# Gathers beside the last batch: at most two under way

## The chip, the cores and the metric

The kernel runs on one core of a Trainium2 chip. The metric is the time of one execution on the device in microseconds, as a median of several runs. Before the change it is 834.48 us (three runs, 833.97 to 837.61). TensorE (PE) multiplies matrices, VectorE (DVE) and ScalarE (ACT) work element by element, GpSimd (POOL) does small element work and issues the gathers, SyncE (SP) issues most other DMAs.

## The reference

A decoder layer on x of 16 x 56 x 256 (batch, tokens, channels): a linear self-attention, a cross-attention over 1500 context rows with 16 heads, and a feed-forward with routed experts. Each is added to its input and normalised. The part whose data the change concerns is the feed-forward:

```python
rows = mask_idx // H          # 2048 entries
cols = mask_idx % H
vals = jnp.einsum('tk,tks->ts', rw, weighted[top_idx])
xg = xt[:, cols]              # the gather
contrib = jax.ops.segment_sum((xg * vals).T, rows, num_segments=H)
out = xt @ W.T + contrib.T
```

For each of 2048 entries a channel of x (`cols`) is picked for all tokens, multiplied by the routed value of token and entry, and added into the channel `rows`.

## The kernel before

Cross-attention goes batch by batch (b = 0 to 15). A batch has eight head pairs t, taken in four duos. For each pair TensorE transposes the probabilities in three groups of four tiles (L1179, `transposes`), ScalarE copies group 0 and 2 out of PSUM (L1300), and so does VectorE with group 1 in the last batch (L1427); then come TensorE's products with the values (L1193). In between stand the scores of pair t+2 (L1157), VectorE's masked copy of them (L1396) and ScalarE's exponentials (L1288). The copies wait for `values_done` (the values two pairs back) and for their group of transposes in `probsT_in_psum`, both counted up by TensorE. In all batches but the last, TensorE also projects the context of the next batch; the last has room, and there the first half of the tokens (448 of 896) is made ready for the feed-forward. Its x, transposed, is stored to DRAM as `x2T[0]` by ScalarE (L677).

The gathers read that store. The feed-forward works in 16 tiles of 128 entries (j = 0 to 15, `NST` = 16) for each half h of the tokens. Gather j is an indirect DMA that GpSimd issues (L683): it fetches 128 rows of 448 floats, 1792 bytes each and 229,376 in all, into the buffer `xg[j]`. Two neighbouring gathers count up one semaphore, `xg_in[j // 2]`, by 16 each. There is one set of sixteen buffers, filled for h = 0 beside the last batch (L1099 to L1107) and refilled for h = 1 during the feed-forward, each as soon as its product has been read (L1722 to L1724). Buffers 0 to 8 lie in the room of the projections, 9 to 14 in that of the values, 15 in that of the stacked keys, and so the loop waits, on GpSimd, before j = 3 (`k_in`, all key transfers), before j = 9 (`values_done`) and before j = 15 (`scores_in_psum`).

The feed-forward begins with TensorE finishing the last tile's attention output (`late_unit_on_tensor`, L741 and L747, with VectorE between and behind) and the first value products (L1753). For each n = 16 h + j VectorE waits for `xg_in` and for the value product and multiplies them (L1898), ScalarE rounds (L1840), GpSimd or VectorE takes the rest (L1712, L1888), and TensorE scatters the two parts into the channels (L1762). GpSimd's first instruction in this block is the memset of `c_stack1` (L1705).

Of the kernel before, what the change touches and what calls it, by code (L numbers as in the profile page):

```python
# [573 lines left out]
def units_before(half, a):  # L574

    if isinstance(half, int) and half == 0:
        return NU * (1 + a)
    return half * NU2 + NU - NR + a * (NU + NR)
# [40 lines left out]
def expert_room(keep):  # L619

    room = {"room": keep["room"][:], "context": keep["context"][:], "w": keep["wkvT"][:].rearrange("p k m d -> p (k m d)"),
            "v": keep["v_sb"][:, 0].rearrange("p l d -> p (l d)")}
    at = dict.fromkeys(room, 0)

    def take(which, cols, rows=P, dt=None):
        view = room[which][0:rows, at[which]:at[which] + cols]
        at[which] += cols
        return view.bitcast(dt) if dt else view  # L630

    return {
        "pick_r": split(take("room", NST * D), NST),
        "c_stack": take("room", HALF),
        "xg": [take("room", HALF, dt=F32) for j in range(XG_ROOM)] + [take("v", HALF) for j in range(XG_ROOM, NST - 1)]
        + [keep["k_stack"][:].rearrange("p k l -> p (k l)")[:, 2 * BUFS * HALF:(2 * BUFS + 1) * HALF].bitcast(F32)],
        "x2T": split(take("context", 2 * KT * HALF), 2 * KT),
        "x2T_hi": split(take("w", KT * HALF), KT),
        "x2T_lo": split(take("w", KT * HALF), KT),
        "c_lo": take("context", T, rows=E, dt=F32R),  # L640
        "channel_row": take("context", D),
        "col_i": take("context", NST, dt=I32),
        "idx_col": take("context", NST, dt=I32),
        "row_i": take("context", NST, dt=I32),
        "row_f": take("context", NST),
        "expert_row": take("context", E, rows=TT),
    }
# [16 lines left out]
def shares_stack(keep, h):  # L664
    return expert_room(keep)["c_stack"] if h == 0 else keep["c_stack1"][:]
# [14 lines left out]
def gather_on_gpsimd(nc, pool, io, keep, h, j):  # L680

    e = expert_room(keep)
    nc.gpsimd.indirect_dma_start(e["xg"][j], None, io["x2T"][h], bass.IndirectOffsetOnAxis(ap=e["col_i"][:, j:j + 1], axis=0)  # L683
                                 ).then_inc(keep["xg_in"][j // 2], 16)
# [12 lines left out]
def result_on_gpsimd(nc, pool, keep, tile):  # L697
    pool.wait_ge(keep["var_ready"], tile + 1)
    t = slice(tile, tile + 1)
    nc.gpsimd.tensor_tensor(keep["rstd"][:, t], keep["var_eps"][:, t], keep["minus_half"][:, t], ALU.pow).then_inc(keep["rstd_ready"], 1)  # L700

def tables_on_gpsimd(nc, pool, keep):

    e = expert_room(keep)
    channels = keep["channels"]
    nc.gpsimd.iota(e["channel_row"], pattern=[[1, D]], base=0, channel_multiplier=0,
                   allow_small_or_imprecise_dtypes=True).then_inc(channels, 1)
    nc.gpsimd.iota(e["expert_row"], pattern=[[1, E]], base=0, channel_multiplier=0,
                   allow_small_or_imprecise_dtypes=True).then_inc(channels, 1)  # L710
# [186 lines left out]
def cross_attention_phase(nc, io, keep):  # L897
    ctx = ExitStack()
    with ctx:
# [73 lines left out]
        def readers_done(b, c):  # L973

            if b == 1:
                return last_reader(AT_FIRST, c) + 1
            half, a = (b - 2) // 2, b % 2
            return units_before(half, a) + last_reader(AT if a or half == 0 else AT_R, c) + 1
# [5 lines left out]
        with nc.Block() as block:  # L984
# [81 lines left out]
            @block.gpsimd  # L1066
            def _(pool):
                def split_context(b):
                    for c in range(NC):
                        e = slice(c * LC, (c + 1) * LC)  # L1070
                        pool.wait_ge(ctx_in[c], 16 * (b + 1))
                        pool.wait_ge(unit_in_psum, readers_done(b, c))
                        nc.gpsimd.tensor_copy(cT_hi[:, :, e], context[:, :, e]).then_inc(ctx_hi, 1)  # L1073
                        pool.wait_ge(ctx_hi, NC * b + c + 1)
                        nc.gpsimd.tensor_tensor(cT_lo[:, :, e], context[:, :, e], cT_hi[:, :, e].bitcast(F32), ALU.subtract).then_inc(ctx_lo, 1)  # L1075

                for part, (raw, hi, lo) in enumerate(((w_raw, "wT_hi", "wT_lo"), (gate_raw, "gateT_hi", "gateT_lo"))):
                    pool.wait_ge(wT_hi_ready, part + 1)
                    nc.gpsimd.tensor_tensor(keep[lo][:], raw, keep[hi][:].bitcast(F32), ALU.subtract).then_inc(keep["wT_lo_ready"], 1)
                pool.wait_ge(load["bias"], 32)  # L1080
                nc.gpsimd.tensor_tensor(x1[:], x1[:], bo_row.unsqueeze(1).broadcast_to([TT, NT, D]), ALU.add).then_inc(x1_bo_ready, 1)
                nc.gpsimd.memset(keep["minus_half"][:], -0.5).then_inc(keep["half_set"], 1)
                pool.wait_ge(keep["half_set"], 1)
                for a in range(2):
                    split_context(1 + a)
                for i in range(NT - 2):
                    for a in range(2):
                        split_context(2 * i + 3 + a)
                    result_on_gpsimd(nc, pool, keep, i)
                split_context(B - 1)  # L1090
                pool.wait_ge(ctx_lo, NC * B)
                tables_on_gpsimd(nc, pool, keep)
                result_on_gpsimd(nc, pool, keep, NT - 2)

                pool.wait_ge(keep["col_ready"], 1)
                pool.wait_ge(unit_in_psum, units_before(last, 1))
                nc.gpsimd.memset(shares_stack(keep, 0).bitcast(F32), 0.0).then_inc(keep["stack_cleared"], 1)
                pool.wait_ge(keep["x2T_stored"][0], 16)
                for j in range(NST):  # L1099
                    if j == XG_EARLY:  # L1100
                        for p in range(NP):
                            pool.wait_ge(k_in[p], 16 * STACK * B)
                    if j == XG_ROOM:
                        pool.wait_ge(values_done, (B - 1) * NP + 2)
                    if j == NST - 1:
                        pool.wait_ge(scores_in_psum, (B - 1) * NP + 3)
                    gather_on_gpsimd(nc, pool, io, keep, 0, j)  # L1107

            @block.tensor
# [857 lines left out]
```

## Time and profile before

| | us |
|---|---|
| median of the runs | 834.48 |
| lowest, highest | 833.97, 837.61 |
| profiled execution | 835.97 |
| its span | 834.2 |
| TensorE busy | 741.3 (89%) |
| VectorE busy | 513.1 (62%) |
| ScalarE busy | 505.9 (61%) |
| GpSimd busy | 224.4 (27%) |

Times in the rows are microseconds from the start of the span. A row of the instruction list gives start, duration, engine, line, operation, output and inputs, shape, count, and in brackets the idle time of the engine before it with what ended it. "remote" there means that the trace shows no engine of this core as the one that released it, "issue" that it shows nothing that was waited for. The granted clock of TensorE is 1.00 at 2.4 GHz and 0.50 at 1.2 GHz. Matmul ends are modelled, and some matmul records can be missing. An issue of a gather counts as busy on GpSimd only as long as the instruction itself runs; its data moves later on queue q0.

### The profile page before, as it was taken

How to read it: one execution, taken by the hardware profiler on the slowest of the kernel's cores; microseconds unless marked ns; L12 is line 12 of the kernel's file. 1: busy time of each engine (PE TensorE's matmuls, PEld its weight loads, DVE VectorE, ACT ScalarE, POOL GpSimd, SP SyncE). 2: the span in 40 equal slices, each digit the busy share in tenths (PEclk: the TensorE clock that was granted, in tenths of full speed). 3: DMA queues.
4: the chain of work that ended last, by engine and by line, in shares of the span. 5: the costliest groups of instructions: out<-in, count | busy, mean ns of one | idle time of the engine just before them, and what ended most of it. 6: DMA issues, size and time to landing. Idle time of an engine off the chain costs nothing. (4 is left out here: it accounts for less than half of the span.)

```text
span 834.2 us, 18337 instructions
## 1 busy us (share of the span) xinstructions
PE 741.3 (89%) x7341; PEld 621.4 (74%) x7341; DVE 513.1 (62%) x993; ACT 505.9 (61%) x846; POOL 224.4 (27%) x176
## 2 busy tenths in 40 slices
PE   5745599999999999999999999999999999647954
PEld 2434388888888888888888888888888888436743
DVE  2886755565665566657656655666566556735655
ACT  4304157776677676767775776677677767523323
POOL 1020340413133131404040504051313310433633
PEclk9775899999999999999999999999999999959978
DMA  9008977887777778877887788778877755830421
GB/s 231 34 4 249 217 186 178 191 194 194 161 186 161 186 166 203 178 187 165 203 177 189 166 204 177 192 169 199 195 162 186 165 112 121 200 97 2 131 70 44
DMA packets 59891, 134.19 MB, mean 161 GB/s; under 512 B 24936, under 2 KB 43080, under 8 KB 59720
## 3 DMA queue, kind: packets, MB, share of 16 engines
q1 hardware_dynamic: 55632, 124.31, 63.9%
q0 software_dynamic: 2048, 7.34, 3.3%
q10 hardware_dynamic: 2128, 1.38, 0.6%
q8 instruction: 59, 0.97, 0.5%
q14 instruction: 24, 0.20, 0.1%
HBM read 53.50 MB, written 5.57 MB: 71 GB/s over the span
## 5 line engine op out<-in xcount | busy, mean ns | idle before, releaser
L1300 ACT ACTIVATE probsT<-ps_T 125x448 f32<-125x448 f32 x376 | 190.8, 541 | 160.1 <-PE ps_T L1179 144.9
L1396 DVE CUSTOM_DVE_ANT_0 scores<-ps_scores,mask_sb 112x1500 f32<-112x1500 f32 x128 | 219.7, 1717 | 94.6 <-PE ps_scores L1157 86.7
L1179 PE MATMUL ps_T<-ident,scores 112*128 112x112 f32 (+1 forms) x1536 | 196.5, 264 | 18.6 <-ACT probsT L1300 16.1
L1179 PEld LDWEIGHTS ps_T<-ident,scores 112*128 112x128 f32 (+1 forms) x1536 | 169.9, 146 | 54.1 <-ACT probsT L1300 36.9
L1288 ACT ACTIVATE scores<-scores,shift 112x1500 f32<-112x1500 f32 x128 | 197.0, 1541 | 3.7 <-DVE shift L1396 3.1
L1145 PE MATMUL ps_proj<-wkvT,room 128*125 128x256 f32 x1152 | 160.1, 288 | 0.0
L1138 PE MATMUL ps_proj<-room,wkvT 128*128 128x500 f32 x576 | 150.0, 406 | 8.4 <-DVE room L1483 8.4
L1073 POOL CAST room<-ctx_rows 128x1000 fp32r<-128x1000 f32 x45 | 45.8, 1019 | 401.1 <-PE ps_proj L1138 400.5
L1145 PEld LDWEIGHTS ps_proj<-wkvT,room 128*125 128x125 f32 x1152 | 141.8, 186 | 8.9 <-issue 8.1
L1138 PEld LDWEIGHTS ps_proj<-room,wkvT 128*128 128x128 f32 x576 | 106.7, 194 | 27.2 <-issue 8.7
L1157 PE MATMUL ps_scores<-k_stack,q_stack 96*112 96x500 f32 x384 | 118.1, 415 | 2.4 <-issue 1.7
L1075 POOL TENSOR_TENSOR room<-ctx_rows,room 128x1000 fp32r<-128x1000 f32 x45 | 105.5, 2345 | 3.6
L1379 DVE COPY v_sb<-ps_proj 125x512 f32<-125x512 f32 x96 | 66.0, 688 | 62.8 <-PE ps_proj L1145 62.8
L1383 DVE SCALAR_TENSOR_TENSOR room<-ps_proj,xbk,room 128x500 fp32r<-128x500 f32 x96 | 70.9, 739 | 51.2 <-ACT room L1283 50.1
L1193 PE MATMUL ps_out<-probsT,v_sb 125*32 125x112 f32 x3072 | 88.6, 263 | 1.9 <-DVE probsT L1427 1.9
L1283 ACT ACTIVATE room<-ps_proj,xbk 128x500 fp32r<-128x500 f32 x96 | 64.7, 674 | 42.2 <-PE ps_proj L1138 23.8
L1193 PEld LDWEIGHTS ps_out<-probsT,v_sb 125*32 125x32 f32 x3072 | 72.6, 111 | 16.9 <-issue 10.7
L1157 PEld LDWEIGHTS ps_scores<-k_stack,q_stack 96*112 96x112 f32 x384 | 58.1, 178 | 11.6 <-issue 3.6
L1840 ACT ACTIVATE k_stack<-prod 128x448 fp32r<-128x448 f32 x32 | 18.2, 579 | 42.5 <-DVE prod L1898 40.3
L1762 PE MATMUL psC<-k_stack,room 128*128 128x448 f32 x128 | 33.6, 392 | 3.0 <-POOL k_stack L1712 2.9
L281 PE MATMUL psA<-xT,wT 128*128 128x448 f32 x48 | 22.7, 638 | 12.2 <-DMA xT<-in_xT 6.8
L1762 PEld LDWEIGHTS psC<-k_stack,room 128*128 128x128 f32 x128 | 25.0, 201 | 7.5 <-POOL k_stack L1712 4.4
(246 smaller groups left out, 489.5 us busy)
## 6 DMA issues: line engine op xcount, KB each, us to landing
k_stack<-room SPq DMA_DIRECT2D x384, 187.5 KB, 3.9
ctx_rows<-in_ctx SPq DMA_DIRECT2D x48, 500.0 KB, 5.6
mask_sb<-in_mask_BxSxS_ff SPq DMA_DIRECT2D x32, 328.1 KB
q_stack<-q_hi SPq DMA_DIRECT2D x32, 112.0 KB, 5.3
q_hi<-k_stack SPq DMA_DIRECT2D x4, 448.0 KB, 3.8
q_lo<-k_stack SPq DMA_DIRECT2D x4, 448.0 KB, 4.0
q_stack<-q_lo SPq DMA_DIRECT2D x16, 112.0 KB, 5.3
xT<-in_xT SPq DMA_DIRECT2D x2, 448.0 KB, 7.9
```

The costliest lines, as they stand in the source:

```text
L1075: nc.gpsimd.tensor_tensor(cT_lo[:, :, e], context[:, :, e], cT_hi[:, :, e].bitcast(F32), ALU.subtract).then_inc(ctx_lo, 1)
L1138: last = nc.tensor.matmul(ps_proj[:, bank, 0:LC], w, x, start=i == 0, stop=i == len(mm) - 1)
L1145: last = nc.tensor.matmul(ps_proj[0:LT, bank, j * D:(j + 1) * D], w, x, start=i == 0, stop=i == len(mm) - 1)
L1157: last = nc.tensor.matmul(ps_scores[0:PN, c, 0:LC], q_stack[:, a, t], k_stack[0:STACK * PD, t, c * LC:(c + 1) * LC], start=True, stop=True)
L1179: last = nc.tensor.transpose(ps_T[0:wide, (TB * t + k) % 2, j * PN:(j + 1) * PN], scores[:, t % 2, key:key + wide], keep["ident"][0:PN, 0:PN])
L1193: last = nc.tensor.matmul(ps_out[k * PD:(k + 1) * PD, d * PN:(d + 1) * PN], v_sb[0:LT, a, j, t * PD:(t + 1) * PD], probsT[:, t % 2, j], st ...
L1283: nc.scalar.activation(k_hi[:, q * LC:(q + 1) * LC], src, ACT.Identity, bias=keep["xbk"][:, p:p + 1]).then_inc(hi_ready, 1)
L1288: nc.scalar.activation(scores[:, t % 2], scores[:, t % 2], ACT.Exp, scale=-1.0, bias=shift[:, t % 2:t % 2 + 1], accum_out=keep["sums"][:, ...
L1300: nc.scalar.activation(probsT[:, t % 2, k * TC:(k + 1) * TC], ps_T[0:LT, (TB * t + k) % 2, 0:TC * PN].rearrange("p (j n) -> p j n", j=TC), ...
L1379: nc.vector.tensor_copy(v_sb[0:LT, a, 2 * p:2 * p + 2], split(ps_proj[0:LT, bank], 2)).then_inc(unit_out, 1)
L1383: nc.vector.scalar_tensor_tensor(out=k_lo[:, c], in0=ps_proj[:, bank, 0:LC], scalar=keep["xbk"][:, p:p + 1], in1=k_hi[:, c].bitcast(F32), ...
L1396: nc.vector.tensor_tensor_reduce(out=split(scores[:, t % 2], NC), in0=ps_scores[0:PN, :, 0:LC], in1=split(mask_sb[:, a], NC), scale=-1.0, ...
```

## The change

In the loop of the first sixteen gathers GpSimd waits, before every even j from 2 on, until both gathers of the pair ahead have landed.

```diff
@@ -1104,6 +1104,8 @@
                         pool.wait_ge(values_done, (B - 1) * NP + 2)
                     if j == NST - 1:
                         pool.wait_ge(scores_in_psum, (B - 1) * NP + 3)
+                    if j % 2 == 0 and j > 0:
+                        pool.wait_ge(keep["xg_in"][j // 2 - 1], 32)
                     gather_on_gpsimd(nc, pool, io, keep, 0, j)
 
             @block.tensor
```

The loop of the second sixteen (L1722) is not touched.

## Rows read from the trace of the kernel before

**Rows 1.** Busy time in stretches: stretch, length, engines, clock, DMA share, GB/s.

```profile
core 0: us, PE busy (x) PEld busy (x) DVE busy (x) ACT busy (x) POOL busy (x), PEclk, DMA share, GB/s
716.00:722.80 6.80, 5.69 (x42) 4.12 (x40) 5.04 (x14) 3.22 (x6) 3.12 (x3) 1.00 0.92 226
722.80:727.00 4.20, 2.59 (x57) 2.04 (x57) 3.96 (x22) 3.53 (x5) 3.22 (x4) 1.00 0.44 115
727.00:741.40 14.40, 2.19 (x6) 0.92 (x5) 0.00 (x0) 0.00 (x0) 9.20 (x10) 0.52 0.65 175
741.40:751.00 9.60, 8.69 (x75) 7.04 (x76) 6.77 (x20) 5.38 (x10) 0.00 (x0) 0.50 0.01 2
```

**Rows 2.** GpSimd's instructions in order of time, first run of gathers (16).

```profile
716.40 1.22 POOL L683 DMA_INDIRECT room<-x2T,ctx_rows  x1 [2.28 <-DMA x2T<-ctx_rows]
...
719.18 0.95 POOL L683 DMA_INDIRECT room<-x2T,ctx_rows  x1 [0.30 <-issue]
722.86 0.94 POOL L683 DMA_INDIRECT room<-x2T,ctx_rows  x1 [2.74 <-DMA k_stack<-room]
724.11 0.95 POOL L683 DMA_INDIRECT room<-x2T,ctx_rows  x1 [0.30 <-issue]
...
738.00 0.95 POOL L683 DMA_INDIRECT k_stack<-x2T,ctx_rows  x1 [0.30 <-issue]
```

**Rows 3.** TensorE, ScalarE and VectorE in order of time around the gathers.

```profile
727.06 0.45 PE L1179 MATMUL ps_T<-ident,scores 112*128 112x112 f32 x3 [0.99 <-issue]
...
741.44 0.54 ACT L1300 ACTIVATE probsT<-ps_T 125x448 f32<-125x448 f32 x1 [15.11 <-remote]
741.51 0.62 DVE L1427 COPY probsT<-ps_T 125x448 f32<-125x448 f32 x1 [14.64 <-remote]
```

**Rows 4.** Gather queue in windows 718:722 and 724:727: packets, MB, share.

```profile
q0 software_dynamic: 137, 0.54, 53.8%
...
q0 software_dynamic: 128, 0.46, 58.2%
```

**Rows 5.** The microseconds in which the two runs of gathers run out.

```profile
741.00:742.00 1.00, 0.00 (x0) 0.00 (x0) 0.49 (x1) 0.54 (x1) 0.00 (x0) 0.50 0.00 0
...
800.00:801.00 1.00, 0.00 (x0) 0.00 (x0) 0.00 (x0) 0.00 (x0) 0.00 (x0) 0.50 0.13 50
```

**Rows 6.** Last instruction of the cross-attention block, first of the next.

```profile
755.96 0.54 ACT L1327 ACTIVATE outT<-ps_out 128x448 f32<-128x448 f32 x1 [0.80 <-PE ps_out L1193]
...
756.77 0.47 POOL L1705 MEMSET c_stack<- 128x448 f32 x1 [17.83 <-POOLq L984]
```

**Rows 7.** Second run of gathers and the product that follows it.

```profile
778.03 1.09 POOL L683 DMA_INDIRECT room<-x2T,ctx_rows  x1 [3.30 <-DMA x2T<-ctx_rows]
779.42 1.33 POOL L683 DMA_INDIRECT room<-x2T,ctx_rows  x1 [0.30 <-DVE prod L1898]
...
792.45 0.65 PE L1753 MATMUL psC<-c_stack,w_stack 128*128 128x448 f32 x2 [0.91 <-DMA c_stack<-ctx_rows]
...
797.40 0.95 POOL L683 DMA_INDIRECT k_stack<-x2T,ctx_rows  x1 [0.30 <-issue]
801.03 1.16 DVE L1898 TENSOR_TENSOR prod<-psC,room 128x448 f32<-128x448 f32 x2 [11.74 <-issue]
```

**Rows 8.** Busy time and clock where the clock rises, and in the feed-forward's start.

```profile
751.00:752.00 1.00, 0.81 (x7) 0.61 (x5) 0.60 (x2) 0.91 (x2) 0.00 (x0) 0.79 0.00 0
...
756.70:764.00 7.30, 6.25 (x42) 5.41 (x43) 5.03 (x11) 1.11 (x2) 2.76 (x3) 1.00 0.00 0
...
806.00:807.00 1.00, 1.00 (x6) 0.92 (x6) 0.71 (x2) 0.55 (x1) 0.00 (x0) 0.98 0.00 0
```

**Rows 9.** TensorE's first groups of the feed-forward, and one at half clock.

```profile
756.81 1.76 PE L741 MATMUL psC<-fold,outT 128*112 128x64 f32 x16 [0.95 <-PEq L984]
758.38 0.66 PE L1753 MATMUL psC<-room,w_stack 128*128 128x448 f32 x2
759.64 1.13 PE L747 MATMUL psC<-r_norm,sel 112*112 112x128 f32 x8 [0.60 <-DVE r_norm L802]
...
801.71 1.27 PE L1753 MATMUL psC<-c_stack,w_stack 128*128 128x448 f32 x2 [8.62 <-DVE prod L1898]
```

## The prediction, made blind

> **What bounds the kernel now.** I read the page first. Most of the span is the cross-attention of 16 batches, where TensorE is busy 9 tenths and more of nearly every slice; only the last slices fall below that. The change touches nothing before 716 us, so the whole argument lies behind it. The table of stretches shows the hole: from 727.0 to 741.4 us VectorE and ScalarE do nothing, TensorE 2.19 us, at half the clock, while GpSimd issues and the DMA engines are busy 0.65 of the time [rows 1]. The list of GpSimd's instructions says what that traffic is: sixteen gathers in three runs, j=0 to 2 from 716.40, a pause for `k_in` until 722.86, then thirteen in a row, each 0.95 us long with 0.30 us between, the last at 738.00 [rows 2].
>
> The three compute engines are not waiting for the gathered data, since the first product that reads it stands in the next block. The code says what they wait for: ScalarE's copy L1300 waits for a group of four transposes, VectorE's copy L1427 for the next group. By the list in order of time TensorE ran the last of these by 727.5, yet the copies start at 741.44 and 741.51, and the trace names no engine as releaser ("remote") [rows 3]. They start 3.4 us after the last gather is issued, in the first microsecond that has no DMA traffic [rows 2, 3, 5]. So something in the gathers' stream holds up what TensorE should pass on, and lets go when the stream ends. It happens again in the feed-forward: the second sixteen are issued from 778.03 to 797.40, VectorE's product for the second half has its matmuls by 793.1 and starts at 801.03, when the traffic has just run out [rows 5, 7]. That is the ground for expecting anything from the change. It is no proof that the number under way is the cause: three gathers in a row at 716 to 720 held nothing up, and in the second sixteen the engines worked on for about ten microseconds.
>
> Behind the hole the remaining work of the batch takes from 741.44 to 756.50, and 0.27 us later the next block starts on all engines [rows 3, 6].
>
> **The change, part by part.** It adds seven waits to GpSimd, before j = 2, 4, ..., 14, each for both gathers of the pair ahead. No instruction is removed or moved; the second sixteen gathers keep their own code. The register work of a wait is nothing beside what it waits for. What is new is the length of the train. One gather is 64 packets: the two issued at 722.86 and 724.11 make 128 by 727.0, so the second is through at most 2.9 us after its issue [rows 4]. The last one, issued at 738.00, has its traffic behind it by 741.0, 3.0 us; the engines woke at 3.4 [rows 2, 3, 5]; in the second train 797.40 to a little past 800, 2.8 us or somewhat more [rows 5, 7]. I take 3.2 us from issue to the semaphore. The step between two gathers of a pair is 0.95 + 0.30 = 1.25 us, and GpSimd's return from the wait is the 0.25 or so that its other gaps show. One pair costs 1.25 + 3.2 + 0.25 = 4.7 us, where two gathers cost 2.5 us today. The bounds are 2.8 and 3.4 us of landing, so 4.3 and 4.9 us.
>
> The first wait is nearly free: by 722 the stream has moved 137 packets, so j=0 and j=1 (128) are down, and j=2 starts at about 722.6 instead of 719.18; j=3 has to sit out `k_in` until then anyway [rows 2, 4]. From there the pairs start at 722.6 + 4.7k; the seventh (j=14, 15) at 722.6 + 28.2 = 750.8, the last gather at 752.05, done at 753.0. Behind these waits on GpSimd stands nothing of this block, but the block ends for everyone only when GpSimd is through: the memset L1705, the first thing of the next block, comes 0.27 us after ScalarE's last copy of this one, and TensorE starts with it [rows 6, 9]. So GpSimd, ready at 739 today, becomes the engine that can set the block's end: 753.0 + 0.3 = 753.3, against 756.77 now. Gain 3.5 us; with the bounds of the pair 5.9 down to 2.3 us. The DMA that feeds `xg` is then as far as it was: j=0 is read first, j=15 last, some twenty microseconds later.
>
> The Trainium skill, "DMA: Bandwidth & Descriptors", section on the anatomy of one DMA on the software path, gives about 2.0 us fixed plus bytes over 436e3 per us. For the 229,376 bytes of a gather that is an estimate of 2.5 us, a pair of 4.0 us and a block end 4.2 us earlier than mine; the row with 3.0 us decides, and the sum goes by it.
>
> Do the other engines finish by 753? At 727 they have two duos of the batch left, which took 15.06 us, 9.6 of them at half clock [rows 1, 3]. The window from 724.0 holds all 128 packets of j=3 and j=4, so traffic begins over 1.1 us after an issue [rows 2, 4]; I take 1.4. If every pair holds TensorE's signals from there to its last landing (4.45 us), the gap to the next traffic is 1.65 us, and the engines do another half microsecond before they need a signal: 2.1 to 2.2 of 4.7 us, 46%. From 727 to 753.3 that is 12 us of the 15. If the hold doesn't form with two under way, they are done at about 740. So the end is set by GpSimd or very near it: between 753.3 and some 757.
>
> What comes back is the clock. Today TensorE has worked without a break since 742, its clock rose at about 751.4 and the feed-forward starts at full clock [rows 1, 8]. After the change it idles before the block's end, or limps through it; the clock is 1.00 up to 727.0 and 0.52 on average behind it [rows 1], so it falls soon after TensorE runs dry. Two matmuls of 448 columns took 0.66 us at full clock and 1.27 at half, a factor of 1.9 [rows 9]. The first groups of the feed-forward are on the chain: L741 1.76 us, L747 1.13 us [rows 9]. If the clock comes back some 4.5 us after the restart, as after 801.71 [rows 8, 9], only L741 pays, +1.6 us; if it takes nine, as after 742.0, all of TensorE's 6.25 us up to 764 pays, at most 0.9 x 6.25 less the 1.05 us of slack there, +4.6 us [rows 8]. I take L741 and L747, 0.9 x 2.89 = 2.6 us.
>
> Sum: -3.5 + 2.6 = -0.9 us. The profiled execution took 835.97 us (span 834.2), 1.5 us above the median of the runs, 834.48. Against that median: 833.6 us. The second hole (789 to 801) is left as it is, since its train isn't changed.
>
> **Rivals.**
> (a) Faster. The hold is gone, and the clock costs nothing because TensorE works up to the block's end, or the landings are as quick as the lower bound: 3.5 to 5.9 us gained, with nothing given back. Middle 4.7: 829.8 us. For it: the first three gathers held nothing up. Against it: if the hold is gone TensorE is done long before GpSimd, and then it is cold.
> (b) Slower: the hold isn't lifted between pairs. The traffic pauses only from a landing to the next pair's first packets, 1.65 us, and where the hold ended at 741.44 there was no next gather. If that doesn't do, it lasts until the longer train is over: 752.05 + 3.4 = 755.4, then 15.06 us of work: 770.5 against 756.50, +14.0 us, 848.5 us. It decides from the point where the release takes longer than the pause. For it: the hold's start doesn't follow the count under way. Against it: VectorE resumed within a microsecond of the last traffic.
> (c) Slightly slower: the pairs take over 4.9 us, or the hold eats more of each pair than I took, and the block ends at 757 to 759, cold: 0.2 to 2.2 us later plus the 1.6 to 4.6 us of the clock, +2 to +7, middle +4.5: 839 us. The engines that now run beside the gathers can also slow the issue: in the second train, beside a busy VectorE, the first two issues took 1.09 and 1.33 us where 0.95 is the rule [rows 7].
> (d) The count has no bearing: the hold comes and goes with something else. Then GpSimd ends at 753, the others at 756.5 as now, and nothing changes: 834.5 us. The Trainium skill, "SBUF — State Buffer", section on the two separate sides, says that a DMA can't slow a compute operation, which speaks for this. The trace has 14 us in which all three compute engines stand beside nothing but gathers [rows 1], so I trust the row over the rule as far as waiting goes.
>
> **How the numbers follow.** Forecast (GpSimd sets the end, cold start) 0.42; (a) 0.23; (b) 0.12; (c) 0.15; (d) 0.08. The forecast's own range is 830.2 (5.9 gained, 1.6 paid) to 836.8 (2.3 gained, 4.6 paid). The whole range reaches down to 828.0, (a) with its best 5.9 and half a microsecond below, and up to 842.0, the end of (c); left out are (b) and the rim of (a). Half a percent, 4.2 us, is about what a measurement of this kernel can tell from none. Faster by more: most of (a) and the rim of the forecast, 0.25. Slower by more: (b) and most of (c), 0.24. Between: 0.51.
>
> **What would show it.** Right: gathers in pairs 4.3 to 4.9 us apart from 722.6, GpSimd's last at about 752, L741 at 753.3 with its sixteen matmuls in over 3 us at half clock, and copies L1300 and L1427 spread over the stretch and not bunched at its end. The DMA share falls to zero once per pair. Wrong: L741 behind 757, or one long idle stretch of ScalarE up to the last landing (b); a full clock at L741 (a); a second hole of another length, which I took as constant. What would upset it most is a clock that stays up while the hold is gone, and a second hole that moves.

## The result: slower, and the profile after

The changed kernel takes 839.63 us, median of 17 runs (837.93 to 843.29), against 834.67 us (17 runs, 831.67 to 837.61) for the kernel before on the same chip: a ratio of 1.0056, 95% interval 1.0040 to 1.0071, so it is slower by about half a percent, clear of the noise. Forecast were 833.6 us and no measurable difference, with a range of 828 to 842. The profiled execution has a span of 839.5 us where the one before has 834.2, so the two profiles differ by 5.3 us, about as much as the medians. Lines behind L1106 have moved down by two.

GpSimd's instructions in order of time, kernel after (start, duration, engine, line; in brackets the idle time ahead of it and what ended it):

```profile
716.75 1.25 POOL L683 DMA_INDIRECT room<-x2T,ctx_rows  x1 [2.95 <-DMA x2T<-ctx_rows]
718.30 0.95 POOL L683 DMA_INDIRECT room<-x2T,ctx_rows  x1 [0.30 <-issue]
723.32 0.94 POOL L683 DMA_INDIRECT room<-x2T,ctx_rows  x1 [4.07 <-DMA room<-x2T,ctx_rows]
724.57 0.95 POOL L683 DMA_INDIRECT room<-x2T,ctx_rows  x1 [0.30 <-issue]
728.14 0.94 POOL L683 DMA_INDIRECT room<-x2T,ctx_rows  x1 [2.63 <-DMA room<-x2T,ctx_rows]
...
752.09 0.94 POOL L683 DMA_INDIRECT v_sb<-x2T,ctx_rows  x1 [2.60 <-DMA v_sb<-x2T,ctx_rows]
753.34 0.95 POOL L683 DMA_INDIRECT k_stack<-x2T,ctx_rows  x1 [0.30 <-issue]
757.60 0.47 POOL L1707 MEMSET c_stack<- 128x448 f32 x1 [3.31 <-POOLq L984]
```

The waits are there: two gathers, then GpSimd idles until both have landed, 4.07 us after the first pair and 2.4 to 2.7 us after the others. From 723.32 to 752.09 are six pairs of 4.80 us. Against the train of before [rows 2] it is now 15 us longer. The last line is the first thing of the next block, and it stands 3.31 us behind the end of the last gather's instruction, 4.26 us behind its start.

```profile
L984 POOLq DRAIN  x1: 13648/13648/13648, 728.5 to 728.5; - x1
...
L984 POOLq DRAIN  x1: 5480/5480/5480, 751.9 to 751.9; - x1
```

The record begins before the last gather has been issued. Before, it ends at 742.1, which is 4.1 us behind the last issue and 0.7 us behind the last landing (741.39); nobody waited for it there. After, it ends at 757.35, 4.0 us behind the last issue and again 0.7 us behind the landing (756.64), and the memset follows 0.25 us later.

ScalarE in order of time, kernel after, where the hole was [rows 3]:

```profile
726.42 0.54 ACT L1302 ACTIVATE probsT<-ps_T 125x448 f32<-125x448 f32 x1 [0.41 <-PE ps_T L1181]
727.67 0.54 ACT L1302 ACTIVATE probsT<-ps_T 125x448 f32<-125x448 f32 x1 [0.71 <-PE ps_T L1181]
...
739.16 0.55 ACT L1302 ACTIVATE probsT<-ps_T 125x448 f32<-125x448 f32 x1 [1.12 <-PE ps_T L1181]
741.30 0.54 ACT L1329 ACTIVATE outT<-ps_out 128x448 f32<-128x448 f32 x1 [1.59 <-PE ps_out L1195]
```

The wait of 15.11 us [rows 3] is gone. All of ScalarE's copies go through, none waits more than 2.14 us from 724 us on, those that wait are released by TensorE, and the last copy of the batch starts at 741.30 instead of 755.96 [rows 6]: the three compute engines have finished the batch 14.7 us earlier. And none of it arrives, as the list of TensorE shows:

```profile
739.05 2.14 PE L1195 MATMUL ps_out<-probsT,v_sb 125*32 125x112 f32 x48
757.64 3.22 PE L741 MATMUL psC<-fold,outT 128*112 128x64 f32 x16 [16.44 <-PEq L984]
760.62 1.09 PE L1755 MATMUL psC<-room,w_stack 128*128 128x448 f32 x2
761.93 2.05 PE L747 MATMUL psC<-r_norm,sel 112*112 112x128 f32 x8 [0.21 <-DVE r_norm L802]
```

It waits 16.44 us for the block to end, starts 0.83 us later than before [rows 9], and then does the same three groups at half speed: 3.22, 1.09 and 2.05 us where it was 1.76, 0.66 and 1.13 [rows 9]. The stretches of the kernel after say how long (stretch, length, busy times of PE, PEld, DVE, ACT, POOL, clock, DMA share, GB/s):

```profile
742.00:744.00 2.00, 0.00 (x0) 0.00 (x0) 0.00 (x0) 0.00 (x0) 1.25 (x2) 1.00 0.00 0
744.00:746.00 2.00, 0.00 (x0) 0.00 (x0) 0.00 (x0) 0.00 (x0) 0.64 (x1) 0.53 0.66 170
746.00:757.00 11.00, 0.00 (x0) 0.00 (x0) 0.00 (x0) 0.00 (x0) 3.78 (x4) 0.50 0.33 94
757.00:764.00 7.00, 6.15 (x27) 5.57 (x28) 2.01 (x4) 1.11 (x2) 1.38 (x2) 0.50 0.00 0
764.00:766.00 2.00, 2.00 (x10) 1.81 (x10) 1.81 (x6) 0.00 (x0) 1.36 (x2) 0.85 0.00 0
```

TensorE is out of work at 741, its clock is at the lower of its two levels (1.2 of 2.4 GHz) from about 744, and it comes back at about 765, 7 us after the restart. In the first stretch there is no DMA traffic, although a gather was issued at 742.44.

All the rest can be followed with four marks on each profile: the first gather, the start of the last block (the memset), the first gather of the second sixteen, the end of the span. All runs made for this study in one table (us; distances between the marks, so that it doesn't matter when an execution reached the first one):

| kernel | first gather to block | block to second gathers | second gathers to end | last gather of first train to block |
|---|---|---|---|---|
| before | 40.4 | 21.3 | 56.2 | (18.8) |
| after | 40.9 | 24.8 | 57.1 | 4.26 |
| e1_warm | 40.8 | 20.9 | 56.7 | 4.44 |
| e2_slide | 33.3 | 26.6 | 56.2 | 4.11 |
| e3_drain | 33.3 | 23.2 | 56.1 | (10.7) |
| e4_second | 40.4 | 21.6 | 54.7 | (18.8) |
| e5_endwait | 41.3 | 26.4 | 56.2 | 5.02 |
| e6_inter | 36.7 | 26.7 | 52.5 | (14.5) |
| e7_drain_both | 35.7 | 23.3 | 51.1 | (10.6) |
| e8_triples | 38.0 | 26.6 | 56.2 | 4.09 |
| e9_moved | 34.7 | 26.4 | 56.1 | 4.12 |
| e10_moved4 | 26.5 | 27.0 | 52.0 | 3.89 |

In brackets: the compute engines, not GpSimd, were last at the block's end. From before to after: +0.35 at the first gather itself, +0.48, +3.50 and +0.97, together the 5.3 us.

Each row is one profiled execution. The times of the runs are medians, and each ratio below is to the kernel before on the same chip (835.38 us there for e1 to e4, 835.45 for e5 to e8, 835.70 for e9 and e10); kernels from different groups are compared by these ratios.

### The profile page after: what moved, and what is told of

Same layout as the page of the kernel before. It is cut to its first block and busy times, and to the rows that moved or that the text cites. A ratio compares the mean times of both kernels' runs of the same rounds, so it can differ in the third digit from the quotient of the medians.

```text
span 839.5 us, 18337 instructions
## 1 busy us (share of the span) xinstructions
PE 741.1 (88%) x7341; PEld 622.1 (74%) x7341; DVE 512.6 (61%) x993; ACT 505.8 (60%) x846; POOL 224.2 (27%) x176
## 5 line engine op out<-in xcount | busy, mean ns | idle before, releaser
L1195 PEld LDWEIGHTS ps_out<-probsT,v_sb 125*32 125x32 f32 x3072 | 72.5, 110 | 17.3 <-issue 10.7
```

Source lines behind the costliest of these rows:

```text
L1195: last = nc.tensor.matmul(ps_out[k * PD:(k + 1) * PD, d * PN:(d + 1) * PN], v_sb[0:LT, a, j, t * PD:(t + 1) * PD], probsT[:, t % 2, j], st ...
```

## Experiments

Three questions: what sets the end of the block, what the clock costs, and what makes and lifts the hold. The base of each diff is named, and the diffs are cut to what matters. The runs with `landed` in them (e2, e4, e6, e7, e8, e10) also deal out the semaphores differently: gather j counts up `xg_in[j % 8]`, a train without waits of its own gets one for the gather eight ahead, and the count to wait for is

```
+def landed(h, j):
+    return 32 * h + 16 * (1 + j // 8)
```

`low(n)` is GpSimd's part of the arithmetic for product n.

**e1_warm.** After, and TensorE is kept at work up to the block's end, with 74 matmuls whose result nobody reads:

```
...
+                for _ in range(74):
+                    nc.tensor.matmul(ps_proj[:, 0, 0:HALF], keep["wT_hi"][:, 0, 0:P], ...)
```

> The changed kernel, with 74 matmuls of 448 columns added at the end of TensorE's list for the last batch; they compute nothing that is read and fill the 16 us in which TensorE waits for GpSimd. Theory (the clock): the feed-forward starts at full clock at 757.6 as in the changed kernel, L741 takes 1.8 us and not 3.2, and GpSimd's second gathers begin 21.2 us behind that start, as before the change, and not 24.7. Time 836.0 us against 839.6. Rival (the feed-forward's start lost its 3.5 us to something else than the clock, such as the gathered data arriving late): 839 to 840 us with the clock up.

Measured: 837.87 us (ratio to before 1.0032, 1.0001 to 1.0064). TensorE and the clock (stretch, length, PE busy, clock, DMA share, GB/s):

```profile
741.00:755.00 14.00, 13.70 (x69) 1.00 0.36 100
755.00:764.00 9.00, 8.07 (x52) 1.00 0.00 0
```

The first group of the block is back at its old length:

```profile
754.95 1.76 PE L741 MATMUL psC<-fold,outT 128*112 128x64 f32 x16 [0.30 <-PEq L984]
```

The stretch from block to second gathers shrinks from 24.8 to 20.9 us, so the cold start costs 3.9 us there, and the distance to the block's start, 40.8, stays as it was. TensorE was as busy as can be beside the gathers and the gathers kept their pace. The time shows less: the ratios, 1.0032 against 1.0056, are 2 us apart with overlapping intervals, and 837.87 us is 1.9 over what was expected. So the 3.9 us rest on one profiled execution of each kernel; the stretch is the sharper reading, since it leaves out what varies elsewhere.

**e5_endwait.** After, and GpSimd also waits for the landing of the last pair before it leaves the block:

```
+                pool.wait_ge(keep["xg_in"][NST // 2 - 1], 32)
```

> The changed kernel with one wait more: at the end of its list beside the last batch GpSimd also waits for the last pair of gathers to have landed, before the block ends. Theory 1, the end of the block waits for the landing of the last gather anyway: the added wait takes over what the profile now shows as 3.31 us in front of the memset, the memset still starts about 4.3 us after the last gather's issue (753.34 to 757.60), and the time stays where the changed kernel's is, about 839.6 us. Rival, the 3.3 us are a fixed price of ending a block after gathers that does not depend on the landing: it comes on top, the memset starts about 7.5 us after the last issue, and the time is about 842.5 us.

Measured: 841.63 us (1.0068, 1.0043 to 1.0094), not to be told from the 1.0056 of after. GpSimd, last gather and memset:

```profile
752.35 0.95 POOL L683 DMA_INDIRECT k_stack<-x2T,ctx_rows  x1 [0.30 <-issue]
757.37 0.47 POOL L1708 MEMSET c_stack<- 128x448 f32 x1 [4.07 <-POOLq L984]
```

```profile
L984 POOLq DRAIN  x1: 1380/1380/1380, 755.7 to 755.7; - x1
```

Behind the six pairs ahead of it this wait costs 2.5 to 2.7 us of idle time; here it moved the memset by 0.8 us (5.02 us from the last issue instead of 4.26). So the two overlap: without any wait in the code, GpSimd's block doesn't end before its last gather is down. In the ten other runs besides this one and the changed kernel the DRAIN ends 0.5 to 0.7 us behind the last landing, while from issue to landing it took 3.1 to 3.5 us.

**e9_moved.** After, and the last pair is issued in the next block, behind the memset:

```
-                for j in range(NST):
+                for j in range(NST - 2):
...
+                for j in range(NST - 2, NST):
+                    if j % 2 == 0:
+                        pool.wait_ge(keep["xg_in"][j // 2 - 1], 32)
+                    gather_on_gpsimd(nc, pool, io, keep, 0, j)
```

> The changed kernel with its last pair of gathers (14 and 15) issued behind the memset in the last block instead of beside the last batch. Theory, the end of the block waits for the landing of the last gather of GpSimd's list, and the list is as long as its pairs: the memset starts one pair (4.8 us) earlier after the first gather, 36.0 us instead of 40.85, again about 4.3 us after the last gather beside the batch; ScalarE and VectorE are done at 741 to 742 and don't set it. The pair in the last block lies in GpSimd's idle time before its first low part. TensorE's clock stays at 0.50 at the block's start, so the stretch to the second gathers stays at 24 to 25 us. Time 839.6 less 4.8, about 834.8 us. Rival, the 3.3 us in front of the memset hang on something other than the gathers: the memset moves by less than 2 us and the time is 838 to 840.

Measured: 836.22 us (1.0004, 0.9982 to 1.0027). By the ratios that is about 4 us under after, and the intervals don't touch.

```profile
748.16 0.94 POOL L683 DMA_INDIRECT v_sb<-x2T,ctx_rows  x1 [0.30 <-issue]
752.28 0.47 POOL L1705 MEMSET c_stack<- 128x448 f32 x1 [3.17 <-POOLq L984]
752.95 0.95 POOL L683 DMA_INDIRECT v_sb<-x2T,ctx_rows  x1 [0.20 <-issue]
```

The first line's instruction was gather 13. The block starts 34.7 us after the first gather instead of 40.9: 4.8 for the pair, and of the other 1.3 the first pair makes 0.9, since its landing was waited for 3.10 us here and not 4.07. The distance from last gather to memset is the same 4.1 us. That confirms the theory and refutes the rival. My 24 to 25 us for the next stretch was wrong: it took 26.4, as in four other runs with a cold start (26.4 to 26.7), and so the time came out 1.4 us over what was expected.

**e2_slide.** Before, and in the first train each gather waits for the one two ahead of it, so at most two are under way as in after, but the stream never empties:

```
+                    if j >= 2:
+                        pool.wait_ge(keep["xg_in"][(j - 2) % 8], landed(0, j - 2))
```

> The first sixteen gathers with at most two under way, but sliding: each waits for the one two ahead of it, not each pair for the pair. The semaphores are dealt out as j modulo 8 for that. The traffic then never pauses for long. Theory A (the hold needs three gathers under way): no hold; one gather per (3.4 + 0.25) / 2 = 1.8 us, last issue near 746, block end at its landing near 750, so 7.5 us earlier than the changed kernel, 832 us. Theory B (a hold forms under any steady traffic and the pauses between pairs lift it): ScalarE and VectorE stand until the train ends near 749, the rest of the batch takes 12 to 15 us behind it, feed-forward from 762 to 765, 844 to 847 us.

Measured: 833.03 us (0.9969, 0.9940 to 0.9998).

```profile
742.62 0.54 ACT L1333 ACTIVATE outT<-ps_out 128x448 f32<-128x448 f32 x1 [2.72 <-remote]
```

```profile
746.84 0.94 POOL L687 DMA_INDIRECT k_stack<-x2T,ctx_rows  x1 [1.37 <-DMA v_sb<-x2T,ctx_rows]
750.95 0.47 POOL L1711 MEMSET c_stack<- 128x448 f32 x1 [3.17 <-POOLq L988]
```

The longest wait on "remote" is this 2.72 us, though there was traffic throughout: the DMA share from 727 to 741 is 0.45 and TensorE was busy 10.46 of those 14 us at full clock. So it isn't the pauses of the changed kernel that freed the engines; a train with two under way holds nobody for longer. Its gathers are also further apart (one every 1.77 us, DMA share 0.45 against 0.65 before), and no run separates the number from the rate. The same limit costs 7.6 us less when it slides, since a gather no longer waits for the one right ahead of it. The block starts 7.1 us earlier than in the kernel before (33.3 against 40.4), and the cold start takes 5.3 of that back (26.6 against 21.3).

**e3_drain.** Before, with a single wait, ahead of gather 8, for all the gathers issued so far:

```
+                    if j == 8:
+                        pool.wait_ge(keep["xg_in"][j // 2 - 1], 32)
```

> The kernel before the change with a single wait: before j = 8 GpSimd waits until j = 6 and 7 have landed. Thirteen gathers in a row become five and eight. Theory (a pause of the traffic lifts the hold): ScalarE's and VectorE's copies start near 731, in the pause, and not at 741; a second hold forms with the eight and ends at 744 to 745. Feed-forward from 756 to 759, time 834 to 837 us. Rival (a hold once formed lasts to the end of the train): copies at 744.6, feed-forward from 760, 838 us.

Measured: 831.21 us (0.9953, 0.9923 to 0.9983), 2.8 us under the range that was expected.

```profile
732.15 0.54 ACT L1302 ACTIVATE probsT<-ps_T 125x448 f32<-125x448 f32 x1 [3.18 <-PE ps_T L1181]
...
733.45 0.94 POOL L683 DMA_INDIRECT room<-x2T,ctx_rows  x1 [2.55 <-DMA room<-x2T,ctx_rows]
...
742.20 0.95 POOL L683 DMA_INDIRECT k_stack<-x2T,ctx_rows  x1 [0.30 <-issue]
752.89 0.47 POOL L1707 MEMSET c_stack<- 128x448 f32 x1 [9.74 <-POOLq L984]
```

The copy starts near 731, as the theory had it, and not at 744. One pause of 2.55 us gives the engines a stretch of work (from 733 to 740 VectorE is busy 5.81 us, where it was idle before), a second, shorter hold forms behind it (from 740 to 745 it is busy 0.28 us), and the block starts 7.1 us earlier. Here the engines set its end, so TensorE arrives there at work and the next stretch is 23.2 us.

**e8_triples.** Before, with the first train in bursts of three, all ahead landed before each:

```
+                    if j in (3, 6, 9, 12, 15):
+                        for i in range(max(j - 8, 0), j):
+                            pool.wait_ge(keep["xg_in"][i % 8], landed(0, i))
```

> First train in threes: gathers 3, 6, 9, 12 and 15 wait for all ahead of them, so up to three are under way; second train as before. Theory 1, what holds TensorE's signals is a backlog that a pause lifts: no waits of ScalarE or VectorE over 4 us in the first train, engines done about 741 to 743. Theory 2, the third gather under way is enough to hold them: several waits of 3 us or more, one in each burst, engines done about 748. Pace: six bursts of about 1.25+1.25+3.2+0.5 = 6.2 us, five of them full, so the last gather is issued near 720+5*6.2+1 = 752, or 747 if three overlap better than two do; block start 4.3 us later, 751 to 756. Time 834 to 839 us.

Measured: 837.73 us (1.0015, 0.9993 to 1.0037).

```profile
742.96 0.54 ACT L1336 ACTIVATE outT<-ps_out 128x448 f32<-128x448 f32 x1 [1.91 <-PE ps_out L1202]
```

No hold with three under way either: the longest wait of ScalarE for a copy is 2.50 us and the batch is done at 742.96. It takes a longer dense run. Five in a row begin to show: 3.18 us for ScalarE in e3_drain, and in e7_drain_both, below, 2.72 us for ScalarE and 2.95 for VectorE, both on "remote". Within the eight behind the pause of e7_drain_both ScalarE waits 6.02 us.

**e4_second.** Before, with the first train as it was; in the second, each gather waits for the one two ahead:

```
                     pool.wait_ge(prod_ready, j + 1)
+                    if j >= 2:
+                        pool.wait_ge(keep["xg_in"][(j - 2) % 8], landed(1, j - 2))
```

> The kernel before the change in its first sixteen gathers, and the second sixteen sliding with two under way. Theory A (the hold needs three under way): VectorE's first product of the second half starts at about 793 and not 801; the last gather is issued near 806, GpSimd's parts of that half come 5 us late behind it, so 3 to 6 us of the 8 are left, 829 to 832 us. Theory B (steady traffic is enough for the hold): it lasts to the end of the longer train, 809, and the time is 842 us.

Measured: 833.52 us (0.9973, 0.9940 to 1.0006), not to be told from before, and over the 829 to 832 of theory A.

```profile
793.45 1.16 DVE L1906 TENSOR_TENSOR prod<-psC,room 128x448 f32<-128x448 f32 x2 [2.84 <-issue]
```

```profile
809.09 0.95 POOL L687 DMA_INDIRECT k_stack<-x2T,ctx_rows  x1 [0.31 <-issue]
810.06 4.45 POOL L1718 TENSOR_TENSOR k_stack<-prod,k_stack 128x448 fp32r<-128x448 f32 x4
```

```profile
PE psC L1770 <- POOL k_stack L1718: 8.5, 1, 8.5
```

The product stands 13.8 us after the second train's start instead of 23.0 [rows 7], so the second hole goes the same way as the first. But GpSimd's own share of the arithmetic is queued behind the longer train, and TensorE waits 8.5 us for it (last line: engine and line, what it waited for, us in total, times, longest). Of 9.2 us only 1.5 arrive.

**e6_inter.** e4_second, with those low parts put between the last gathers:

```
+                    for n in {12: POOL_FIRST[0:1], 14: POOL_FIRST[1:3]}.get(j, ()):
+                        low(n)
```

> First train as before, held as before. In the second train each gather waits until the one two ahead of it has landed, and GpSimd's low parts of the last four k-blocks are made between the gathers (one before gather 12, two before gather 14, one after the last). With gathers alone spaced, VectorE's product came at 793.5 instead of 801 but GpSimd's parts at 810, and nothing was gained in sum. If the theory holds that TensorE's completion signals are held only under dense gathers and that the queue on GpSimd ate the gain: product at about 793, no wait of VectorE or TensorE on GpSimd's parts above 3 us, time about 828 us (827 to 831 by 834.5 less 4 to 8). Rival, the end is set by the landing of the last gathers and not by GpSimd's queue: the waits of 8 us stay under another name and the time is about 834.

Measured: 830.87 us (0.9946, 0.9921 to 0.9971; runs from 826.21 to 836.56). The stretch from second gathers to end falls from 56.2 to 52.5 us and the long wait on GpSimd is gone. The profiled execution shows something else: its first train, whose waits reach eight gathers back, held ScalarE for 6.5 us at most (11.4 us in three waits), and the block started 36.7 us after the first gather. The first train's code is that of e4_second, where the block started 40.4 us after the first gather. So how long the hold lasts isn't the same in every execution of a dense train, which may be why these runs scatter.

**e7_drain_both.** Before, with the pause of e3_drain in the first train and the second train of e6_inter:

> One pause in the first train (before gather 8 all eight ahead have landed), and the spaced second train with GpSimd's low parts between the gathers. The pause alone gave 831.2, about 4 us less than before on that chip. If the two gains are apart from each other, the time is that of the spaced second train less 4: about 824 us where that gains 6, 830 where it gains nothing. Rival, the earlier start of the last block is eaten by a colder TensorE clock: both together are no better than the better one alone.

Measured: 826.17 us, four runs (0.9882, 0.9844 to 0.9920). The gains add up: 1.2% here, 0.5% each for e3_drain and e6_inter alone; the stretches are 35.7, 23.3 and 51.1 us.

**e10_moved4.** Before, with the sliding first train, whose last four gathers go into the next block, and the second train of e6_inter:

```
-                for j in range(NST):
+                for j in range(NST - 4):
...
+                    for j in {0: (NST - 4, NST - 3), 2: (NST - 2,), 3: (NST - 1,)}.get(n, ()):
+                        pool.wait_ge(keep["xg_in"][(j - 2) % 8], landed(0, j - 2))
+                        gather_on_gpsimd(nc, pool, io, keep, 0, j)
```

> All that the runs showed put together: in the first train each gather waits for the one two ahead, its last four gathers go into the last block (two before GpSimd's first low part, two between the next ones), and the second train is spaced with GpSimd's low parts between its gathers. If the end of the block is the later of the engines (done at about 743) and the landing of gather 11 (issued about 738 in the run with the same spacing, plus 4.1 us), the last block starts at about 745 instead of 751; TensorE's clock is at 0.50 there, so 25 to 26 us to the second gathers, near 771, and 51 us from there to the end: about 822 us, or 818 if the clock stays up because the gap before the block is short. Rival, the four gathers delay GpSimd's low parts or slow the last block: the stretch to the second gathers grows by what was gained and the time stays near 826.

Measured: 822.75 us, four runs (0.9846, 0.9818 to 0.9873), 13 us below before and, by the ratios, some 17 below after.

```profile
738.86 0.94 POOL L687 DMA_INDIRECT v_sb<-x2T,ctx_rows  x1 [1.29 <-DMA v_sb<-x2T,ctx_rows]
742.75 0.47 POOL L1709 MEMSET c_stack<- 128x448 f32 x1 [2.94 <-POOLq L988]
743.42 0.95 POOL L687 DMA_INDIRECT v_sb<-x2T,ctx_rows  x1 [0.20 <-issue]
...
758.27 1.09 POOL L687 DMA_INDIRECT k_stack<-x2T,ctx_rows  x1 [0.18 <-issue]
759.39 4.46 POOL L1716 TENSOR_TENSOR k_stack<-prod,k_stack 128x448 fp32r<-128x448 f32 x4
```

```profile
742.79 1.76 PE L745 MATMUL psC<-fold,outT 128*112 128x64 f32 x16 [1.69 <-PEq L988]
```

Now the last landing and the last work of the batch meet: TensorE waits 1.69 us for the block instead of 16.44, and the batch's gain arrives. The clock still dips (0.50 from 746 to about 752). Gather 15, at 758.27, stands ahead of four low parts and delays them: VectorE waits 5.07 us at 762.91 for what cost 3.73 us in e9_moved. The stretch is 27.0 us against 26.4, although the clock is at 0.50 for less of it (13.7 against 16.3 us). That fits the rival of the expectation at the size of about a microsecond; no run isolates it.

## Why the prediction was wrong, point by point

**The hold.** Right, and better than taken. With two under way it doesn't form; the engines' last copy starts at 741.3, near the prediction's "about 740". The estimate that they get only 46% of each pair was needless. Rival (b), a hold that lasts to the train's end, fell with it, and so did (d). The Trainium skill, "SBUF — State Buffer", section on the two separate sides, which spoke for (d), isn't touched as far as the speed of an operation goes: VectorE's copy takes 0.62 us inside the traffic and outside. But what was late here were not operations, it was their start.

**The pair.** Taken as 4.7 us from 722.6; it was 4.80 from 723.32. Six pairs make 0.6 us, the later start 0.7. A small error, inside the bounds given. The estimate of 4.0 us a pair, from the Trainium skill, "DMA: Bandwidth & Descriptors", section on the anatomy of one DMA on the software path, would have been off by 0.8 us each.

**The end of the block: the step that failed.** The prediction had the last gather issued at 752.05, "done 753.0", and the block's end 0.3 us behind it. 753.0 is the end of the instruction that issues the gather, not of the gather. The row I leaned on, 0.27 us from ScalarE's last copy to the memset [rows 6], is the price of a block's end when everybody else has long been through; at that time GpSimd's last gather had been down for 15 us, and the row can't show what an outstanding one costs. Another row of the same trace could: the DRAIN that ends at 742.1, 4.1 us behind the last issue. By it the block's end would have been 752.05 + 4.1 + 0.25 = 756.4, and the gain 0.4 us and not 3.5. Measured is 4.26 us from the last issue, where 1.25 was taken: 3.0 us too little. e5_endwait shows that a wait for the landing overlaps with it, e9_moved that it travels with the last gather, and five more runs without an added wait have it at 3.9 to 4.4 us. With 0.7 and 0.6 from the pairs, the gain of 3.5 us became a loss of 0.8.

**The clock.** Mechanism right, size low. 2.6 us were taken, with 1.6 to 4.6 as bounds; e1_warm gives 3.9 us, before against after 3.5. The assumption that only L741 and L747 pay was wrong: the clock came back 7 us after the restart. In five other runs the stretch was 5.1 to 5.4 us longer than in the kernel before, beyond the upper bound. There the clock came back only 9.5 to 9.9 us after the restart and fell again later in the stretch for 6.8 us, where before and after have 3.4 us at that place. The time at 0.50 within the stretch orders all runs but e10_moved4:

| at 0.50 within the stretch, us | stretch, us | kernels |
|---|---|---|
| 0.0 | 20.9 | e1_warm |
| 3.4 | 21.3, 21.6 | before, e4_second |
| 6.8 | 23.2, 23.3 | e3_drain, e7_drain_both |
| 10.4 | 24.8 | after |
| 16.3 to 16.8 | 26.4 to 26.7 | e2, e5, e6, e8, e9 |

**The second hole.** Taken as constant. From the second train's start to VectorE's product it was 23.1 us after (782.36 to 805.45) and 23.0 before [rows 7], so that held. Behind the product the changed kernel took 0.9 us longer (34.1 against 33.2); e5_endwait, which has the same train and one wait more, shows nothing of it (56.2 us from second gathers to end, as before). The clock rows suggest a cause: from the product on the clock stays at 0.50 for another 7.0 us in after, 5.0 in before and 4.3 in e5_endwait, and from the product to the end it is 34.1, 33.2 and 32.8 us. No run isolates it.

Sum: +0.8 for the block's start (with 0.35 of it at the first gather), +3.5 for the clock, +0.9 behind the product, where the prediction had -3.5 and +2.6. The time that came out is that of rival (c), "slightly slower", 839 us; its block end of 757 to 759, cold, is what happened. Its reason was a different one, though: neither did the pairs take over 4.9 us, nor did the hold eat into them. I gave it 0.15, since I had priced the landing of the last gather at nothing.

**What stays open.** Why a dense run of gathers from GpSimd keeps TensorE's results from being seen by the others. That it does, the semaphore events of the trace of before show: the transposes that end at 725.98 are counted up at 741.36, 15.4 us later, while the last counts of VectorE and ScalarE ahead of the hole, up to 726.4, come within 0.1 us of their instructions' ends. A rival, that the engines had run out of instructions to execute, finds no support: the only queue with packets from 727 to 741 is that of the gathers (packets, MB, share),

```profile
q0 software_dynamic: 702, 2.52, 66.4%
```

and the queues of kind "instruction" have no packet before 745, when the engines are long at work again. The runs bound the hold (nothing over 3.2 us under bursts of up to five, 6 us under eight, 15 us under thirteen) and show what lifts it (one pause of 2.5 us); no run separates the number of gathers from the time they are dense, or tells whether gathers from another queue do the same.

## What to carry to other kernels

A gather issued from GpSimd's list isn't over for a block when its instruction is: count its landing before the block's end (the end of the engine's DRAIN shows it, also where nobody waits for it yet), and put the last ones behind the boundary if their readers are there. A limit on transfers under way should slide (each waits for the one two ahead), since waiting in pairs pays the whole round trip every second time; and whatever arithmetic stands behind the longer train on the same engine has to be placed between its members. Before counting a gain, look which engine reaches the next barrier last after it, and whether TensorE will be cold there.

## What the runs showed of the hardware, unexpected

- A block doesn't end on GpSimd before the gathers it issued have landed, with no wait written: its DRAIN ends 0.5 to 0.7 us behind the last landing in all eleven kernels without such a wait. Where GpSimd is last, the next block's first instruction comes 3.9 to 4.4 us after the last issue in six kernels, 5.0 with a wait written.
- Three gathers of 224 KB in a row leave the other engines alone (no wait over 2.5 us for ScalarE's copies in e8_triples); thirteen in a row kept ScalarE and VectorE waiting for 15 us, and a single pause of 2.55 us took this apart. One dense train of the same code was held for 6.5 us at most in one execution.
- Cold starts of the same work differed: 24.8 us in the changed kernel, 26.4 to 26.7 in five runs, 20.9 kept warm. TensorE's idle time ahead doesn't order them: 16.4 us in the changed kernel, 10.4 to 16.8 us in four of the five, and in the fifth, e6_inter, 0.95 us behind nine microseconds of work at half clock. The time at 0.50 behind the start does: 0, 10.4, and 16.3 to 16.8 us.
- With each gather waiting for the one two ahead, there is one every 1.77 us (723.84 to 746.84 in thirteen steps, e2_slide); in closed pairs one every 2.40 us; without waits one every 1.25 us.
